# A vision tower on one core: one wait moved, v in wide split pieces, two tiles finished apart, output weights centred and scaled

## The reference

```python
# layer 0, token block
qkv = h @ w_qkv
q, k, v = jnp.split(qkv, 3, axis=-1)
attn = jax.nn.softmax(jnp.einsum('bhid,bhjd->bhij', q, k) * scale, axis=-1)
o = jnp.einsum('bhij,bhjd->bhid', attn, v)
...
# layer 1, attention
out = out * gate
out = out @ Wo
out = _layernorm(out, ln_w, ln_b)      # (x - mean) * rsqrt(var + eps) * ln_w + ln_b
...
h = _layernorm(h + out, axis=-1)
...
# layer 1, feed-forward: the patch tokens
patch_out = _gelu(patch_tokens @ moe0_W1 + moe0_b1) @ moe0_W2 + moe0_b2
```

## Time and profile before

| | |
|---|---|
| median of 3 runs | 416.32 us (416.05 to 422.2) |
| profiled execution, its own time | 418.84 us |
| its span, first to last instruction | 417.0 us |
| TensorE busy | 398.4 us, 96% of the span |
| VectorE, ScalarE, GpSimd busy | 57%, 41%, 12% |
| mean granted TensorE clock | 0.987 of full speed |

### The profile page before, as it was taken

How to read it: one execution, slowest core, us unless ns; L and a number is a source line. 1 busy time by engine, 2 the same in 40 slices (tenths; PEclk the granted TensorE clock), 3 DMA queues, 4 the chain that set the end, 5 groups by cost and what they waited for, 6 DMA issues and landing times.

```text
span 417.0 us, 7793 instructions
## 1 busy us (share of the span) xinstructions
PE 398.4 (96%) x3100; PEld 332.8 (80%) x3100; DVE 239.5 (57%) x734; ACT 171.4 (41%) x290; POOL 50.8 (12%) x107
## 2 busy tenths in 40 slices
PE   8999999998899999999999989999999999999993
PEld 8978888787568767686747778998998999869783
DVE  1567656613368676777456387576558304687353
ACT  1246441742466546453513663354233320551420
POOL 7134010340000000100001310000000200304002
PEclk9999999999999999999999999999999989999998
DMA  7999600000299000000000997044221000000001
GB/s 200 260 194 223 142 11 1 2 0 4 61 242 283 12 2 0 2 0 2 2 0 11 272 265 221 17 128 132 67 67 57 2 0 2 3 2 2 2 0 38
DMA packets 28658, 30.53 MB, mean 73 GB/s; under 512 B 4868, under 2 KB 24074, under 8 KB 28623
## 3 DMA queue, kind: packets, MB, share of 16 engines
q1 hardware_dynamic: 28072, 29.82, 29.1%
q10 hardware_dynamic: 390, 0.22, 0.2%
q0 software_dynamic: 160, 0.01, 0.0%
HBM read 29.63 MB, written 0.39 MB: 72 GB/s over the span
## 4 chain that ended last, share of the span: by engine, by line
PE 83%; DVE 7%; ACT 3%; DMA 2%; issue 2%; POOL 1%; SPq 0%; DVEq 0%; POOLq 0%
PE ps L1474 75%; PE ps L1478 7%; DMA front<-in_x 2%; PE ps L1486 2%; DVE bn L984 1%; DVE wide L1349 1%; POOL rstd L509 1%; DVE mv L987 1%; ACT front L670 1%; DVE xn L999 1%; DVE front L1136 0%; DVE front L1135 0%; ACT front L686 0%; ACT front L766 0%; DVE front L1129 0%
## 5 line engine op out<-in xcount | busy, mean ns | idle before, releaser
L1474 PE MATMUL ps<-halves 128*128 128x512 f32 (+1 forms) x360 | 80.5, 378 | 1.3 <-ACT front L716 1.3
L1474 PE MATMUL ps<-front 64*64 64x64 f32 (+3 forms) x912 | 71.7, 265 | 5.1 <-ACT front L772 1.4
L1474 PEld LDWEIGHTS ps<-front 64*64 64x64 f32 (+2 forms) x912 | 64.9, 166 | 13.8 <-issue 4.4
L1474 PE MATMUL ps<-wide,front 128*128 128x192 f32 x432 | 73.7, 332 | 0.0
L1474 PEld LDWEIGHTS ps<-halves 128*128 128x128 f32 x360 | 63.0, 188 | 13.1 <-ACT front L716 1.7
L1474 PEld LDWEIGHTS ps<-wide,front 128*128 128x128 f32 x432 | 72.0, 194 | 1.0 <-issue 0.5
L716 ACT ACTIVATE front<-ps,colc 128x512 f32<-128x512 f32 x60 | 39.6, 688 | 53.0 <-PE ps L1474 52.9
L1478 PE MATMUL ps<-ident,front 128*128 128x128 f32 (+1 forms) x192 | 28.6, 276 | 0.7 <-DVE front L1149 0.4
L1296 DVE SCALAR_TENSOR_TENSOR xn<-ps,small,xn 128x192 f32<-128x192 f32 x28 | 9.8, 410 | 29.7 <-PE ps L1474 29.7
L1478 PEld LDWEIGHTS ps<-ident,front 128*128 128x128 f32 (+1 forms) x192 | 21.2, 138 | 6.3 <-issue 3.0
L1474 PE MATMUL ps<-xT,turned 128*64 128x256 f32 (+1 forms) x96 | 24.0, 474 | 1.5 <-ACT turned L656 1.5
(11 more groups left out here) (268 smaller groups left out, 537.9 us busy)
## 6 DMA issues: line engine op xcount, KB each, us to landing
wide<-in_w SPq DMA_DIRECT2D x8, 576.0 KB, 4.6
wide<-in_w SPq DMA_DIRECT2D x8, 384.0 KB, 6.0
wide<-in_w SPq DMA_DIRECT2D x16, 192.0 KB, 6.3
front<-in_a2w SPq DMA_DIRECT2D x5, 576.0 KB
front<-in_a1w SPq DMA_DIRECT2D x5, 384.0 KB
front<-in_x SPq DMA_DIRECT2D x3, 512.0 KB, 7.8
front<-in_w_qkv SPq DMA_DIRECT2D x2, 576.0 KB, 7.5
front<-in_a1w SPq DMA_DIRECT2D x5, 192.0 KB
```

Source lines behind the costliest of these rows:

```text
L1474: return pe.matmul(o, l, r, start=start, stop=stop)
```

## The change

- The wait for wt_act of all four experts goes from before project1(0, 0) to before project1(0, 1).
- v of head pairs 3, 4 and 5 is no longer computed pair by pair in plain f32. The v weights of these pairs (384 columns) are split too (wvx, two more ScalarE copies in heads_high(1), two more VectorE subtractions after heads_low(1)); values_wide(i) computes one token tile for all three pairs by five fp32r matmuls of 384 columns. Tiles 0 and 1 are done in the iteration hp = 2 (before and after project0), tiles 2 and 3 in hp = 3; in hp = 4 there is no v product. The transfer of the weights' second group carries v's last 64 rows once more (for the low part).
- The second attention's output weights are centred over their output channels and multiplied by ln_w once (wos), on VectorE, before the last expert's weighted sum. TensorE multiplies the gated output by wos too, into banks 6 and 7, in place of 15 of 25 keep_busy matmuls; joined reads this product, and scaled is gone.
- Of the last feed-forward product each tile is signalled by itself (y_tile), tile 3 goes to bank 6, and tiles 2 and 3 are added, normed and centred one by one; image 7 is sent by SP instead of ScalarE's queue.

```diff
-                                     (wqkv[DB:P, 1, 0:2 * H * DH0], slice(P, D), 2)):
+                                     (wqkv[DB:P, 1, 0:(2 + g) * H * DH0], slice(P, D), 2 + g)):
...
+            sp.wait_ge(s["fin_ready"], 5)
+            send(sp, B - 1)
...
+                if g == 1:
+                    act.activation(wvx.high, heads_of(wqkv[:, 0], 3, g)[:, 2], ACT.Copy)
+                    act.activation(wvx.both, heads_of(wqkv[:, 1], 3, g)[:, 2], ACT.Copy).then_inc(s["wv_hi"], 1)
...
+            def v0_wide(i):
+
+                act.wait_ge(s["v0_mm"], 3 + i + 1)
+                act.activation(v0w[:, i, :], ps[:, 2, 0:3 * P], ACT.Copy).then_inc(s["v0_done"], 1)
...
             for hp in range(PAIRS):
+                if hp in (2, 3):
+                    v0_wide(2 * hp - 4)
                 if hp + 1 < PAIRS:
                     q0_out(hp + 1)
-                    v0_out(hp + 1)
+                    if hp + 1 < 3:
+                        v0_out(hp + 1)
+                    elif hp in (2, 3):
+                        v0_wide(2 * hp - 3)
...
                 if hp == 0:
                     heads_low(1, slice(0, 3 * P), "wx_lo")
+                    dve.wait_ge(s["wv_hi"], 1)
+                    dve.tensor_tensor(wvx.low, heads_of(wqkv[:, 0], 3, 1)[:, 2], wvx.high.bitcast(F32), ALU.subtract)
+                    dve.tensor_tensor(wvx.both[DB:P], heads_of(wqkv[DB:P, 1], 3, 1)[:, 2],
+                                      wvx.both[DB:P].bitcast(F32), ALU.subtract).then_inc(s["wv_lo"], 1)
...
             weights_low(w3x, wqk3, 4)
+            dve.wait_ge(s["s3_in"], 16 * 20)
+            dve.wait_ge(s["pad_made"], 4)
+            for c in range(2):
+                link(dve.bn_stats(bn[:, c, :], wvo3[:, 1, c, :]))
+                link(dve.bn_aggr(mv[:, c, :], bn[:, c, :]))
+                ins = dve.scalar_tensor_tensor(wos[:, c, :], wvo3[:, 1, c, :], mv[:, c, 0:1], bc["ln_w"][:, :],
+                                               ALU.subtract, ALU.mult)
+            ins.then_inc(s["wos_made"], 1)
+            dve.wait_ge(s["wos_made"], 1)
...
             def joined(g):
                 deviation()
+                dve.wait_ge(s["zw_mm"], g + 1)
                 for i in (2 * g, 2 * g + 1):
-                    ins = dve.scalar_tensor_tensor(tok[:, i, :], tok[:, i, :], rstd[:, i:i + 1], xn[:, i, :],
+                    ins = dve.scalar_tensor_tensor(tok[:, i, :], two_t(6, i), rstd[:, i:i + 1], xn[:, i, :],
                                                    ALU.mult, ALU.add)
                 link(ins)
...
-            finish(0)
+            added(0, 2)
+            moments(of(tok), 0)
+            centre(of(tok), of(xn), 0, done="fin_ready")
             dve.wait_ge(s["cls_mm"], 1)
...
-            finish(1)
+            added(2, 1)
+            moments_one(2)
+            added(3, 1)
+            moments_one(3)
+            centre_one(2)
+            centre_one(3)
...
+            def values_wide(i):
+
+                pe.wait_ge(s["wv_lo"], 1)
+                pe.wait_ge(s["v0_done"], 3 + i)
+                at, o = slice(i * P, (i + 1) * P), ps[:, 2, 0:3 * P]
+                mm(o, xs0.high[:, at], wvx.high, True, False)
+                mm(o, xs0.high[:, at], wvx.low, False, False)
+                mm(o, xs0.both[:, at], wvx.both, False, False)
+                mm(o, xs0.low[:, at], wvx.high, False, False)
+                mm(o, xs0.lowB[:, at], wvx.both, False, True).then_inc(s["v0_mm"], 1)
...
             for hp in range(PAIRS - 1):
+                if hp in (2, 3):
+                    values_wide(2 * hp - 4)
                 project0(hp + 1)
-                values_in0(hp + 1)
+                if hp + 1 < 3:
+                    values_in0(hp + 1)
+                elif hp in (2, 3):
+                    values_wide(2 * hp - 3)
                 turn0(hp)
                 scores0(hp + 1)
                 values0(hp)
...
-                if x == 0 and e == 0:
+                if x == 1 and e == 0:
                     pe.wait_ge(s["wt_act"], EA)
-                if x == 1 and e == 0:
                     pe.wait_ge(s["wt_dve"], EA)
                     pe.nop().then_inc(s["mixer_left"], 1)
...
-            keep_busy(25, 2)
-            turn_part(xn, 0, 5, (6, 7))
+            pe.wait_ge(s["wos_made"], 1)
+            for i in range(NT):
+                for k in range(2):
+                    ins = mm(two_t(6, i), xT[:, k, i * P:(i + 1) * P], wos[:, k, :], k == 0, k == 1)
+                if i % 2:
+                    ins.then_inc(s["zw_mm"], 1)
+            keep_busy(10, 2)
+            turn_part(xn, 0, 5, (4, 5))
```

More of the change, by code:

```diff
@@ L137, in vit_tower @@
         mx0 = take(2, B)
+        v0w = take(NT, 3 * P)
         take = carve(front[:, 9600:])
@@ L197, in vit_tower @@
         wqkx = Split(halves[:, 0:HALF], 2 * H * DH0)
+        wvx = Split(halves[:, HALF + 4 * T:HALF + 4 * T + 9 * P], 3 * P)
         wffx = Split(halves[:, HALF + 4 * T:HALF + 4 * T + 3 * MLP], MLP)
@@ L288, in vit_tower @@
             gate1_mm gate1_done gate3_mm gate3_done gate3_out q3_mm q3_done v3_mm v3_done
[L289 removed]
+            e3_mm e3_done pv3_mm og_done decay_exp decay_done dist_ready wos_made zw_mm
             xg_done cl_mm cl_sub cl_exp selm_done hc_mm hc_done hct_mm hct_done yc_mm yc_done cls_mm
[L291 to L292 removed]
+            wx_first wv_hi wv_lo k1_first w1_hi w1_lo xs_hiA xs_hi xs_lo wx_hiA wx_hi wx_lo bpatch_in
+            y_tile fin_ready sel_made pad_made dve_step pool_step """.split()
         s = {n: sem(n) for n in names}
@@ L482, in _ @@
             tell(pool.memset(a2bc, 0.0), "consts_made")
-            for v in (wqkv[DB:P, 1, 2 * H * DH0:], gw[DB:P, 1, :], vw[DB:P, 1, :], gwc[DB:P, 1, :, :],
+            for v in (wqkv[DB:P, 1, 2 * H * DH0:2 * H * DH0 + 3 * P], gw[DB:P, 1, :], vw[DB:P, 1, :], gwc[DB:P, 1, :, :],
                       wvo3[DB:P, 0, 1, :]):
@@ L501, in _, with rsqrt @@
             lns = [0]
-            def rsqrt(g, rows=P, n=2):
+            def rsqrt(g, rows=P, n=2, first=None):
                 lns[0] += 1
-                i = slice(2 * g, 2 * g + n)
+                first = 2 * g if first is None else first
+                i = slice(first, first + n)
                 pool.wait_ge(s["var_ready"], lns[0])
@@ L589, in _ @@
             rsqrt(0, 96, 1)
-            rsqrt(1)
+            rsqrt(1, n=1)
+            rsqrt(1, n=1, first=3)
         @block.scalar
@@ L1367, in branch @@
                 return two_t(4, i)
-            def scaled(g):
-                for i in (2 * g, 2 * g + 1):
-                    ins = dve.scalar_tensor_tensor(tok[:, i, :], branch(i), mv[:, i, 0:1], bc["ln_w"][:, :],
-                                                   ALU.subtract, ALU.mult)
-                link(ins)
             def joined(g):
                 deviation()
+                dve.wait_ge(s["zw_mm"], g + 1)
                 for i in (2 * g, 2 * g + 1):
-                    ins = dve.scalar_tensor_tensor(tok[:, i, :], tok[:, i, :], rstd[:, i:i + 1], xn[:, i, :],
+                    ins = dve.scalar_tensor_tensor(tok[:, i, :], two_t(6, i), rstd[:, i:i + 1], xn[:, i, :],
                                                    ALU.mult, ALU.add)
@@ L1384, in _ @@
                 moments(branch, g)
-                dve.wait_ge(s["var_ready"], lns[0] + g + 1)
-                scaled(g)
-                if g == 0:
-                    dve.wait_ge(s["bias_added"], 3)
+            dve.wait_ge(s["bias_added"], 3)
             for g in range(2):
@@ L1776, in up_rest, with down @@
                     jobs[0] += 4
-            def down(h, w, bank, halves=False, tiles=range(NT)):
+            def down(h, w, bank, halves=False, tiles=range(NT), each=False):
                 for i in tiles:
+                    o = ps[:, 6, 0:D] if each and i == 3 else two_t(bank, i)
                     for f in range(NF):
-                        ins = mm(two_t(bank, i), h[:, f, i * P:(i + 1) * P], w[:, f, :], f == 0, f == NF - 1)
-                    if halves and i % 2:
+                        ins = mm(o, h[:, f, i * P:(i + 1) * P], w[:, f, :], f == 0, f == NF - 1)
+                    if each:
+                        ins.then_inc(s["y_tile"], 1)
+                    elif halves and i % 2:
                         ins.then_inc(s["y_half"], 1)
-                if not halves:
+                if not halves and not each:
                     ins.then_inc(s["y_mm"], 1)
@@ L2145, in _ @@
             pe.wait_ge(s["m0_in"], 64)
-            down(hT[:, 0], m0w2, 4, halves=True, tiles=range(2))
+            down(hT[:, 0], m0w2, 4, tiles=range(2), each=True)
             pe.wait_ge(s["selm_done"], 1)
@@ L2155, in _ @@
             ins.then_inc(s["cls_mm"], 1)
-            down(hT[:, 0], m0w2, 4, halves=True, tiles=range(2, NT))
+            down(hT[:, 0], m0w2, 4, tiles=range(2, NT), each=True)
 _INS = {
```

45 lines of the change are left out of this document (25 added, 20 removed).

## The result

| | before | after |
|---|---|---|
| median of 20 runs each, same chip | 418.40 us (415.73 to 422.65) | 414.82 us (412.65 to 416.57) |
| ratio of the two, 95% interval | | 0.9924 [0.9905, 0.9942] |
| profiled execution: time, span, mean granted clock | 418.84, 417.0, 0.987 | 415.73, 414.0, 0.987 |

By the ratio the change wins 3.2 us (2.4 to 4.0) where 4.1 were forecast; the two medians alone are 3.6 us apart. The three runs of before that the forecast started from had a median of 416.32, two microseconds under the median of twenty. On their level the measured ratio gives 416.32 * 0.9924 = 413.2, one microsecond above the forecast's 412.2; on the level of the twenty runs the forecast's own ratio would have given 414.2.

The account below looks back on a forecast made before the run. The prediction took TensorE, busy 96% of the span, as the bound. Its terms, -3.0 - 0.7 - 0.2 - 0.2 = -4.1 us, gave ratio 0.990 on the median 416.32, so 412.2 us; range 410.3 to 415.0.

Parts of the forecast that it names:

- Without the rest ahead of it I expect the clock to stay: First expert's projection: with TensorE's 1.47 us stop gone, full clock stays, saving about 1.52 us lost at 1.2 GHz.
- if the clock falls elsewhere instead: Stated sign of a wrong prediction: the half clock near the first projection shows up at another place; no size given.
- the centred weights: Last expert and second attention: +0.6 us for VectorE's added block, -0.8 us at the later join, both -0.2 us.
- The moved wait: First expert's projection: TensorE's 1.47 us stop and the slow clock after it go, -3.0 us.
- the tiles apart: End of the kernel: last two tiles finished separately, fewer transfers in ScalarE's queue, -0.2 us (-0.6 to +0.4).
- Rival 1: First expert's projection: the clock gives nothing back or its slow stretch only moves; -2.6 us, 413.7, chance 0.24.
- The wide v: First attention: 384-column pieces at 0.184 us, gain partly lost waiting for VectorE's softmax; -0.7 us (-1.7 to +0.4).
- The block's cost: Before the last expert's weighted sum: VectorE making the new output weights delays TensorE's turn, +0.6 us (0.3 to 2.0).
- the join's gain: Second attention's layer norm: VectorE's scaling goes, so join and turn come earlier, -0.8 us (0 to -1.6).
- Rivals 3 and 4: 3: first projection held by another condition, 415.2, chance 0.04. 4: 384-column pieces at plain f32 rate, about 420.9, chance 0.03.
- rival 2: First attention and last expert: VectorE becomes the bound, wide pieces gain nothing, block costs its upper half; about 414, chance 0.12.
- rival 5: More won than counted: all of the wide pieces' stream and a covered block of new weights; 410.2, chance 0.07.

Follow-up runs that it names:

- the filler: The kernel before with six multiplications of identities ahead of the wait before the first expert's projection, order of work kept; 0.9976, 416.72 us.
- the second set: The kernel after, unchanged, timed again beside the one without the centred weights; 0.9915 against before, 415.15 us.

## Why the prediction was wrong, point by point

**The step that failed is the clock.** "Without the rest ahead of it I expect the clock to stay" put -1.5 us into the sum, and no other term had a price for the clock. At this place it stays, but in the profile of after a stretch at half clock stands in the second attention instead (from 369.1) and takes 0.83 us back, and the mean clock of after isn't above that of before. The prediction's own sign of being wrong, "if the clock falls elsewhere instead", came. The second term that was off is the centred weights: -0.2 forecast, +0.8 (0.0 to 1.5) measured alone. How the 0.9 us between -4.1 and -3.2 divide between the two isn't settled.

**What a stretch at half clock costs** can be read from the runs themselves. The 89 timed runs of before in four sets have clocks from 0.986 to 0.994, and their time falls by 4.1 us (give or take 0.3) per 0.01 of clock; the correlation is -0.85. One hundredth of a span of 417 us is 4.17 us, so for this kernel the price is about one for one, and the clock goes with most of its spread, 415.7 to 421.3. A stretch of 3.4 us at 0.5 is 0.004 of the span, 1.7 us, and this is what one costs in the last down projections (17.55 for 15.87). It isn't the price everywhere. The 64-column matmuls of the second attention, with their waits, take 2.7 us at full clock (six profiles) and 3.3 to 3.6 with one stretch in or beside them (nine profiles), 0.5 to 0.8 more, because a wait for VectorE of 0.61 us goes in exchange. And over the 12 runs of the centred weights alone the time falls by only 0.4 us (give or take 1.1) per 0.01. The profiles have none to three such stretches while TensorE works.

**The moved wait, -3.0.** In the profile this place gives the 3.0. But the 1.5 us of clock were those of one execution, and one of six profiles with the rest has no fall there. Over the runs the clock rises by 0.0025 with the moved wait and 0.0029 with the filler, which at 4.1 per 0.01 would be 1.0 to 1.2 us. The part gives -2.5, and its interval (-1.6 to -3.6) still holds -3.0.

**Did the clock stay won?** Not in the whole change, and this is what the forecast missed. The mean clock of after is 0.9900 over its 20 runs and 0.9891 in the second set, and that of before is 0.9900 over 76 runs of the other sets and 0.9892 beside that second set: no change. Eight of the eleven profiles with full clock near 103 have a stretch in the second attention (from 365 to 369), and two of the five that fall near 103. Three of the eight have the old output weights: the moved wait, the filler and the tiles apart, each alone. So the stretch there doesn't need the new weights. The centred weights may add to it: the clock is 0.0049 lower (give or take 0.0017) with them alone, which is 4.1 us more at half clock in a run, more than the tails of any two profiles differ by; the 0.0037 in the whole (0.9928 to 0.9891) could be the tail's. Which of the part's edits does it isn't settled. Unread, the block of statistics lowers the clock by 0.0011; with the block earlier and all else of the part, the 16 more matmul records in the second attention too, it is 0.0013. Neither can be told from nothing, and the two don't make up the 0.0049 that both together have at the change's place, but their errors (0.0016 and 0.0017) leave room for it.

Rival 1 said that the clock "only moves", and gave 413.7, -2.6 us. The profiles show that it moves and that half of it stays won. The total of -3.2 lies between rival and forecast; its interval (-2.4 to -4.0) holds the rival's and just misses the forecast's -4.1.

**The wide v, -0.7: its pieces right, its sum not resolved.** The piece took 0.179 for 0.184, the new wait 0.61 for 0.7. Up to the turn of pair 2 0.32 was lost, as forecast (46.46 - 40.00 against 46.31 - 40.17), 0.23 of it a wait for ScalarE's copies. Another 0.5 goes by the turn of pair 3, of which 0.34 is a longer stop of "issue" (0.84 for 0.50), a term that the sum didn't have. The stop comes and goes: 0 to 0.83 us in eight profiles with v as in before, 0 to 0.96 in eight with the wide v. So the profile gives 0.2. Alone it was -0.6, in the whole some -0.8, neither resolved.

**The centred weights, -0.2: both terms right, the total wrong.** The block's cost was 0.68 for 0.6, the join's gain 0.76 for 0.8. The part came to +0.8 alone and +0.6 (not resolved) in the whole. What is missing is argued to be the clock: 0.0037 to 0.0049 at 4.1 us per 0.01 would be 1.5 to 2.0 us, more than the two terms leave. This is an upper end, by the cheaper price in the second attention and by the tail; no kernel shows it alone.

**The tiles apart, -0.2: not contradicted,** -0.4 alone (not resolved), -0.4 in the tail of the profile.

**The level.** The forecast was put on the median of three runs. It noted that the profiled execution stood 2.5 us above it and took this as room for rival 1; it was the three runs that stood low, 2.1 under the median of twenty. So of the 2.6 us by which 414.8 is above 412.2 two are this level and no fault of the mechanism. Rivals 3 and 4 are refuted: the moved wait works, and the wide piece runs at the split rate. Of rival 2 nothing is seen in the profile, where VectorE is waited for 0.61 us and the block costs 0.68, and of rival 5 nothing beyond the sum.

## What to carry to other kernels

When a rest of TensorE goes together with a stretch at half clock, cost the rest from the timeline and the clock from the mean of many runs: one profile shows one draw. Look at the mean granted clock of every version, since an edit with a right sum can lose it elsewhere; the difference times the span is the most that it can have cost, less the part behind TensorE's last matmul. Then look where the stretches stand: the same 3.4 us took 1.7 us in one place and 0.8 in another. Put work of an engine that has slack where the slack is, not just ahead of its next deadline: the same block half an expert earlier was worth 1.7 us in the whole and 2.0 alone, both known to a microsecond or two, 0.7 of it visible on the timeline.

## What the runs showed of the hardware

- The granted clock falls to 0.50 with TensorE busy, too. While TensorE set the time, the falls that the sixteen profiles show began in three places: near 103, behind small transposes and a rest of 1.47 us (five of six profiles with the rest, none of ten without); in or right behind the matmuls of 8 and 3 rows (333 to 339); and in the second attention with its many 64-column matmuls (365 to 373). Each of the three has full clock in one profile and half in the next.
- One such stretch of 3.4 us cost 1.7 us in the last down projections, where TensorE waits for nobody, and 0.5 to 0.8 among the 64-column matmuls, where it otherwise waits 0.61 us for VectorE.
- The clock also stands at 0.50 at the end of the span, behind TensorE's last matmul, for 0.8 to 4.1 us. The mean clock of a run counts this.
- Mixing matmuls of 3 or 8 rows pair by pair between split pieces of 512 columns cost 1.24 us for four interleavings, beyond the work itself.
- TensorE stood still for up to 0.96 us in the first attention with nothing in the profile that it waited for, in twelve of sixteen profiles, with and without the wide v. This stays open.
